# The opening of a graph layer: where row statistics, readiness signals and weight loads stand

## The reference, cut to what matters

```
x = x + gnn(_layernorm(x), src, dst, edge_weight, W, b)      # 12500 nodes x 256, 200000 edges, sorted by dst
    msgs = features[src] * edge_weight[:, None]
    agg  = segment_sum(msgs, dst, 12500)
    out  = einsum('ni,oi->no', agg, W) + b
x = x + ffn(_layernorm(x), ...)                              # graph attention picks 2 of 4 experts per node
    h = x @ W_gat; a softmax over 131072 random edges plus self loops gives expert scores
    out = sum over experts of gate * (gelu(x @ W1[e] + b1[e]) @ W2[e] + b2[e])
```

## Time and profile before

| | |
|---|---|
| runs | 3775.30, 3775.73, 3779.75 us; median 3775.73 us |
| profiled execution | 3777.66 us, of which the span in the profile is 3775.6 us |
| block one | to 109.75 us of the span |
| block two | 109.75 to about 2080 us |
| PE busy | 2982.2 us, 79% |
| POOL busy | 2745.2 us, 73% |
| DVE busy | 1982.0 us, 52% |
| ACT busy | 823.6 us, 22% |
| granted TensorE clock, mean | 0.895 |

### The profile page before, as it was taken

The page is one execution under the profiler, slowest core; times in us unless marked ns, Lnnn a source line. Parts: engine busy times, 40 slices in busy tenths (PEclk is TensorE's granted clock), DMA queues, the critical chain, the costliest instruction groups (busy, mean ns, idle before and its releaser), DMA issues. The chain is left out here.

```text
span 3775.6 us, 58501 instructions
## 1 busy us (share of the span) xinstructions
PE 2982.2 (79%) x13925; PEld 2434.1 (64%) x13926; DVE 1982.0 (52%) x5026; ACT 823.6 (22%) x2338; POOL 2745.2 (73%) x2817
## 2 busy tenths in 40 slices
PE   1465566576867898878888799999999999997348
PEld 1354444454645666666666688888888888886337
DVE  8676667877777666564344223333342434241557
ACT  6300000000111111111222222223232322221147
POOL 6477777777777777777777677777777777777572
PEclk6687778787878999999999899999999999998679
DMA  9533333333333444444444122232222222221279
GB/s 350 175 104 102 105 108 109 106 110 112 113 111 113 120 123 123 123 120 124 128 129 128 47 73 56 55 115 58 71 55 74 56 73 72 54 74 36 65 264 365
DMA packets 276541, 424.61 MB, mean 112 GB/s; under 512 B 59704, under 2 KB 210211, under 8 KB 275363
## 3 DMA queue, kind: packets, MB, share of 16 engines
q0 software_dynamic: 114208, 216.64, 21.7%
q1 hardware_dynamic: 64175, 114.71, 8.3%
q10 hardware_dynamic: 98004, 91.50, 7.5%
HBM read 317.12 MB, written 105.97 MB: 112 GB/s over the span
## 5 line engine op out<-in xcount | busy, mean ns | idle before, releaser
L653 POOL DMA_INDIRECT rows<-feats,src_t x1500 | 1475.0, 983 | 485.3 <-issue 442.2
L1166 POOL DMA_INDIRECT got<-row_dram,src_sorted x1024 | 997.4, 974 | 332.9 <-issue 332.9
L812 PE MATMUL node_sums<-rows,ys_ahead 128*128 x3904 | 995.9, 409 | 285.7 <-SPq L636 133.8
L812 PEld LDWEIGHTS node_sums<-rows,ys_ahead 128*128 128x128 f32 x3904 | 763.8, 202 | 485.5 <-issue 371.1
L1249 PE MATMUL d_hidden<-d_yt,w 128*128 128x256 f32 x3136 | 714.1, 381 | 35.2 <-DVE d_yt L1333 35.2
L1260 PE MATMUL d_expert<-w,hid 128*128 128x256 f32 x3136 | 708.7, 379 | 0.0
L1249 PEld LDWEIGHTS d_hidden<-d_yt,w 128*128 128x128 f32 x3136 | 595.5, 191 | 116.0 <-DVE d_yt L1333 36.0
L1260 PEld LDWEIGHTS d_expert<-w,hid 128*128 128x128 f32 x3136 | 595.8, 190 | 81.0
L1312 DVE TENSOR_TENSOR yo<-d_expert,x_and_b 128x512 f32<-128x512 f32 x196 | 135.5, 692 | 880.2 <-PE d_expert L1260 872.4
L871 DVE TENSOR_SCALAR ys_ahead<-iota,rel,ew_t 128x128 f32<-128x128 f32 x1952 | 558.4, 363 | 64.4 <-DVE rel L867 0.5
L1194 ACT ACTIVATE hid<-d_hidden,b1c 128x256 f32<-128x256 f32 x784 | 326.3, 471 | 1020.1 <-PE d_hidden L1249 845.2
(11 more groups left out here) (303 smaller groups left out, 2185.0 us busy)
## 6 DMA issues: line engine op xcount, KB each, us to landing
y_dram<-yo ACTq DMA_DIRECT2D x196, 256.0 KB, 2.3
ys<-y_dram SPq DMA_DIRECT2D x36, 1024.0 KB, 9.1
rows<-feats,src_t POOLq DMA_INDIRECT x1500, 2.8
got<-row_dram,src_sorted POOLq DMA_INDIRECT x1024
ys_ahead<-y_dram SPq DMA_DIRECT2D x13, 1024.0 KB, 11.0
x_dram<-edge_plan ACTq DMA_DIRECT2D x98, 128.0 KB
d_x<-x_dram ACTq DMA_DIRECT2D x49, 256.0 KB, 2.9
ys_ahead<-in_x ACTq DMA_DIRECT2D x97, 128.0 KB
```

What stands on the lines that cost most here:

```text
L653: pool.indirect_dma_start(rows[:, g % RING, j, :], None, feats, bass.IndirectOffsetOnAxis(ap=m.src_t[:, g * GT + j:g * GT + j + 1], axis=0 ...
L812: t = pe.matmul(psA[:, ds(((code >> 1) & 1) * 512, FEAT)], hot[:, r, j, :], rows[:, ds((code >> 2) & (RING - 1), 1), j, :], start=False, s ...
L1166: pool.indirect_dma_start(got[:, k, j, 0:ROWF], None, m.row_dram, bass.IndirectOffsetOnAxis(ap=m.src_sorted[:, BEGIN[b] + j:BEGIN[b] + j + ...
```

## The change

- `PRE_DONE` falls from 9 to 6: only the first six raw groups are normalised by ACT in block one, the other ten in block two.
- A table `GROUP_AT` places `group_statistics`, `group_deviation` and `group_scale` of all 16 raw groups in block one; the seven sets that stood in block two are gone from there.
- SP opens block two by telling the six ready groups, then issues W (on its own semaphore `s_wr`), the small tensors, and the edge index. It tells groups 6 to 15 as they are normalised. The 14 expert loads and the 8 stores of zeros are issued one by one, each after one of the 16 landings of the ring's next round.
- PE starts turning W on `s_wr` alone and waits for the small tensors afterwards. ACT issues its first load of x at once and copies the turned W before it waits for that load.
- `sort_init` moves from before the first unit's one-hots to behind them.

```diff
-PRE_DONE = 9
+PRE_DONE = 6
+GROUP_AT = [[], [], [], [], [], [0], [1], [2], [3, 4], [5, 6], [7, 8], [9], [10, 11], [12], [13, 14, 15]]
 @block.scalar  (block one)
-                g = n - (CHUNKS - PRE_DONE)
-                if g >= 0:
+                for g in GROUP_AT[n]:
                     group_deviation(act, m, g)
                 normalise(n)
-                if g >= 0:
-                    group_normalise(act, m, g)
+                for g in GROUP_AT[n]:
+                    if g < PRE_DONE:
+                        group_normalise(act, m, g)
+            for g in GROUP_AT[CHUNKS]:
+                group_deviation(act, m, g)
 @block.vector  (block one)
                 scale(n - 1)
                 if n == 5:
                     plan_steps()
-                if g + 1 >= 0 and n < CHUNKS:
-                    group_statistics(v, m, g + 1)
-                if g >= 0:
+                for g in GROUP_AT[n]:
+                    group_statistics(v, m, g)
+                for g in GROUP_AT[n - 1]:
                     group_scale(v, m, g)
+            for g in GROUP_AT[CHUNKS]:
+                group_scale(v, m, g)
 @block.sync  (block two)
-            (edge index x2, W, wg, brow, att x2, 14 expert loads, wait s_pc, 8 stores of zeros)
-            for g in range(RING):
+            for g in range(PRE_DONE):
                 sp.wait_ge(m.s_gn, g + 1)
                 sp.sem_inc(s_ready, 1)
+            (W -> s_wr, wg, brow, att x2 -> s_w, edge index x2)
+            for g in range(PRE_DONE, RING):
+                sp.wait_ge(m.s_gn, g + 1)
+                sp.sem_inc(s_ready, 1)
+            sp.wait_ge(s_pc, PC)
+            for k in range(RING):
+                sp.wait_ge(s_got[k], 2 * 16 * GT)
+                sp.sem_inc(s_ready, 1)
+                if k < HALVES + FB + 2 * EXPERTS:
+                    expert_load(k)
+                if k >= RING - 8:
+                    sp.dma_start(flat[k - (RING - 8)], zeros[:]).then_inc(s_zo, 16)
-            with sp.Fori(1, full_rounds) as i:
+            with sp.Fori(2, full_rounds) as i:
 @block.scalar  (block two)
-            act.wait_ge(s_w, 16 * 5)
             load(0, 0)
+            act.wait_ge(s_wt, 1)
+            act.copy(w_t[:], ...).then_inc(s_wte, 1)
             act.wait_ge(s_xin, 16)
             load(1, 1)
-            act.wait_ge(s_wt, 1)
-            act.copy(w_t[:], ...).then_inc(s_wte, 1)
-            for g in range(PRE_DONE, RING):
-                group_deviation(act, m, g)
             for g in range(PRE_DONE, RING):
                 group_normalise(act, m, g)
 @block.tensor  (block two)
-            pe.wait_ge(s_w, 16 * 5)
+            pe.wait_ge(s_wr, 16)
...
             pe.wait_ge(s_wte, 1)
             pe.wait_ge(s_pc, PC)
+            pe.wait_ge(s_w, 16 * 4)
 @block.vector  (block two)
-            for g in range(PRE_DONE, RING):
-                group_statistics(v, m, g)
-            for g in range(PRE_DONE, RING):
-                group_scale(v, m, g)
-            sort_init()
             buf = 2
             for n in range(UNITS):
                 with v.Fori(CUT[n], CUT[n + 1]) as u:
                     ...
+                if n == 0:
+                    sort_init()
```

More of the change, by code:

```diff
@@ L446, in _ @@
                     statistics(n)
-                g = n - 1 - (CHUNKS - PRE_DONE)
                 scale(n - 1)
@@ L564, in weighted_sums @@
         s_pc = sem("b_pool_const")
+        s_wr = sem("b_w_loaded")
         s_w, s_wt, s_wte = sem("b_weights"), sem("b_w_turned"), sem("b_w_ready")
@@ L605, in _ @@
         def _(sp):
-            sp.dma_start(key_i[0], edge_index[1, :].rearrange("(p j) -> p j", p=P)).then_inc(s_ei, 16)
-            sp.dma_start(key_i[1], edge_index[0, :].rearrange("(p j) -> p j", p=P)).then_inc(s_ei, 16)
-            sp.dma_start(w_raw[:], W.rearrange("(o p) i -> p o i", p=P)).then_inc(s_w, 16)
+            for g in range(PRE_DONE):
+                sp.wait_ge(m.s_gn, g + 1)
+                sp.sem_inc(s_ready, 1)
+            sp.dma_start(w_raw[:], W.rearrange("(o p) i -> p o i", p=P)).then_inc(s_wr, 16)
             sp.dma_start(wg[:], W_gat.rearrange("(k p) c -> p k c", p=P)).then_inc(s_w, 16)
@@ L613, in _ @@
                              ).then_inc(s_w, 16)
[L614 to L629, removed]
-            for g in range(RING):
+            sp.dma_start(key_i[0], edge_index[1, :].rearrange("(p j) -> p j", p=P)).then_inc(s_ei, 16)
@@ L631, in _, with expert_load @@
+            sp.dma_start(key_i[1], edge_index[0, :].rearrange("(p j) -> p j", p=P)).then_inc(s_ei, 16)
+            for g in range(PRE_DONE, RING):
                 sp.wait_ge(m.s_gn, g + 1)
                 sp.sem_inc(s_ready, 1)
-            with sp.Fori(1, full_rounds) as i:
+            def expert_load(k):
+                if k < HALVES:
+                    sp.dma_start(m.w1[:, k, :, :], W1[:, k * P:(k + 1) * P, :].rearrange("e p n -> p e n")
+                                 ).then_inc(s_experts, 16)
+                elif k < HALVES + FB:
+                    k -= HALVES
+                    sp.dma_start(m.w2[:, k, :, :], W2[:, k * P:(k + 1) * P, :].rearrange("e p n -> p e n")
+                                 ).then_inc(s_experts, 16)
+                elif k < HALVES + FB + EXPERTS:
+                    k -= HALVES + FB
+                    sp.dma_start(m.b2r[:, k, :], b2[k:k + 1, :].to_broadcast([P, FEAT])).then_inc(s_experts, 16)
+                else:
+                    k -= HALVES + FB + EXPERTS
+                    with nc.allow_non_contiguous_dma(reason="a bias of 8 KB, once"):
+                        sp.dma_start(m.b1c[:, k, :], b1[k, :].rearrange("(k p) -> p k", p=P)).then_inc(s_experts, 16)
@@ L634, in _ @@
+            flat = m.adst_first.rearrange("(q p n) c -> q p (n c)", q=8, p=P)
+            sp.wait_ge(s_pc, PC)
[7 more added lines that the diff above has]
+            with sp.Fori(2, full_rounds) as i:
                 for k in range(RING):
@@ L738, in _ @@
             act.sem_inc(s_evac, 1)
-            act.wait_ge(s_w, 16 * 5)
             load(0, 0)
+            act.wait_ge(s_wt, 1)
+            act.copy(w_t[:], psX[:, :].rearrange("p (k o) -> p k o", k=HALVES)).then_inc(s_wte, 1)
             act.wait_ge(s_xin, 16)
             load(1, 1)
-            act.wait_ge(s_wt, 1)
-            act.copy(w_t[:], psX[:, :].rearrange("p (k o) -> p k o", k=HALVES)).then_inc(s_wte, 1)
-            for g in range(PRE_DONE, RING):
-                group_deviation(act, m, g)
             for g in range(PRE_DONE, RING):
@@ L1047, in _ @@
                     sort_end(buf)
-            v.wait_ge(s_w, 16 * 5)
+            v.wait_ge(s_w, 16 * 4)
             for q in range(len(TERMS) - 1):
```

## The result

| | before | after |
|---|---|---|
| runs beside each other, first job | median 3775.74 us (6) | median 3760.0 us (3755.51 to 3766.28, 6) |
| ratio | | 0.9958, 95% interval 0.9945 to 0.9971 |
| second job | 3778.07 us (15) | 3762.12 us (5), ratio 0.9960 (0.9947 to 0.9974) |
| third job | 3778.16 us (15) | 3760.37 us (5), ratio 0.9952 (0.9939 to 0.9966) |
| spans in the profiles | 3775.6, 3774.8 us | 3759.5, 3756.3, 3758.4 us |

The changed kernel is 15.7, 16.0 and 17.8 us faster in the three jobs. I forecast 18.6 us faster, 3757.1 us, in a range of 3753 to 3763. The first profile of it took 3761.89 us with a span of 3759.5.

What follows compares the result with a forecast made beforehand. POOL's unbroken gathers were taken to bound block two, so the first refill's start counts. Terms 1.9 − 20.7 + 0.25 = −18.6 us take the median from 3775.73 to 3757.1 us, range 3753 to 3763.

Steps and rivals of the forecast that it cites:

- reading of the bound: Block two: POOL gathers without a pause from its first refill and ends the block, so that refill's start counts.
- Term one: End of block one: DVE's extra statistics make ACT wait before its last chunks, +1.9 us, bounds 0 and +5.
- Term two: Opening of block two: first refill at +11.2 us from the block's start instead of 31.9, −20.7 us, bounds −19.5 and −21.5.
- Term three: Block two: `sort_init` on DVE now runs beside POOL's gathers and slows a few, +0.25 us, bounds 0 and 5.6.
- The sum: Whole kernel: 1.9 − 20.7 + 0.25 = −18.6 us, median 3757.1 us.
- The cover: Block two: moved normalisations, expert loads and `sort_init`'s delay of `hots` stay hidden; some 21 us remain before POOL's refill.
- (a): Block one takes DVE's extra 14.1 us whole, leaving a gain of 6.6, 3769 us; chance 0.04.
- (b): Block two: `sort_init` stops POOL for its 5.6 us, leaving a gain of 13.2, 3762.5 us; chance 0.05.
- (c): Block two: the moved loads slow POOL's refills by 23.5 us, +4.9 in all, 3780.6 us; chance 0.03.
- (d): Block two is closed by something other than POOL, so the earlier start gains nothing, 3775.7 us; chance 0.02.

Runs made afterwards that it cites:

- reordered only: Changed kernel with block one and the seven groups' statistics as before, only block two's opening reordered: median 3759.41 us, beside 3762.12 for the changed kernel.
- burst: Changed kernel with the 14 expert loads and 8 stores issued in one go behind the edge index, before telling groups 6 to 15: median 3760.26 us.

## Why the prediction was right

Its reading of the bound held: POOL gathers without a pause from its first refill, PE's early waits of 8 and 10 us (reordered only, burst) passed POOL by, and the time followed the first refill.

- **Term one, +1.9 us.** Measured +1.3 in the first profile, +1.7 in the mean. The mechanism is the predicted one: ACT's wait of 2.95 us for DVE's last statistics. DVE's last work was expected at 108.4 and ended at 107.7.
- **Term two, −20.7 us.** Measured −20.66 in the first pair of profiles, −19.9 in the mean. The new opening was forecast at 11.2 us and took 11.1 to 11.6. That it came so close is in part luck. I had the last small tensor hold the opening of the banks until +5.9, and the first step 0.7 behind it. The banks opened at +5.22, +5.47 and +5.35 in the three profiles, in the first on ACT's copy and not on a tensor, and the first step came 1.45 to 1.49 later, with 1.0 us of idle time on PE that my sum did not have. The two errors, −0.5 and +0.75, nearly cancel. What I did not see is that the *old* opening varies: SP's issues of loads set it, and 31.93 was its long case beside 30.51. The 0.8 us between is part of what the totals lack.
- **Term three, +0.25 us.** Here the size was off: the first 50 gathers lost 1.2 us in the mean, 1.4 in the first profile. I priced `sort_init` by one gather of 1.10 us; the casts gave 0.2 each, and one gather was held by the OR for 0.7 us more. The step that failed is the choice of the nearest row: no row of before had a two-input operation of that length beside a gather, though its gathers beside the one-hots of the counts, two-input operations of 0.66 us, took up to 1.15 us. Even by my row the sum was short: 5.6 us hold four gathers at a pitch of 1.29, and four times 0.15 is 0.6, not 0.25. The bounds of 0 to 5.6 held it.
- **The sum.** −18.6 was forecast for the path up to the last gather; the first pair of profiles has −18.1 there, the means −16.1. A part of the rest is the 2.9 us from the 51st gather to the last by which the third profile of the changed kernel is longer; they are slower gathers all along, without a pause, and why they are slower is open. Behind the last gather nothing is lost on average; single executions differ by 3 us in block four. Two slips of the working do not bear on the sum: W's way adds up to +5.3 and not +5.2, and +5.3 to +6.5 for the tensor gives bounds of −20.1 and −21.3 for term two, so that −19.5 and −21.5 are wider than their rows.
- **The cover.** The refill behind the first `hots` had about 21 us in hand by my walk; `hots` started at 152.32 and the next step's matmul at 179.02 (forecast 153.3 and 179.9), and none of POOL's waits came back. The ten normalisations, the told groups and the spread loads cost nothing, and even the burst did not.
- **The rivals.** (a) three sets under the last chunk and ACT's relief left 1.7 and not 14.1 us. (b) 1.2 us and not 5.6. (c) shown false by the burst. (d) did not happen.

## What to carry to other kernels

Find the one queue that runs without a pause to the end of a stage and ask only when its first element starts; signals that need no work go ahead of loads that nobody awaits, and each wait should name only what its next instruction reads. Work that moves out of a stage with slack into one where two engines share the path can cost more than it frees: here the statistics cost 1.7 us in block one and cost nothing in block two once SP's order was mended (11.45 us to the first refill with them, 11.14 to 11.55 without). Where single executions differ by 3 us, compare marks in several profiles of both kernels, early marks above all, before a missing microsecond is given to the change.

## What was not expected of the hardware

- A gather that began 0.39 us into an int32 OR of 1.23 us with two inputs took 1.66 us instead of 0.95; those that began 0.15 us before an OR took 0.95. Beside casts of 0.69 us gathers took 1.15 us.
- Gathers issued in 0.95 us beside 14 loads and 8 stores in flight.
- From the 51st gather to the 1500th it took 1862.26 to 1868.85 us in thirteen profiles, with no pause between gathers; the difference is in their own durations.
- The landing of a small tensor behind W varied: PE waited for it until 4.9 us after its issue in one profile, and in the first profile of the changed kernel it had landed within 3.1 us, before PE looked for it.
- In block four a gap of PE of 2.75 us instead of 1.54 was followed by a granted clock of 0.83 over 10 us and 8.74 us for 32 matmuls instead of 7.14; in the second profile of before the same stood at 0.87 and 8.83 us.
